# Order of VectorE, GpSimd and ScalarE work in the expert loop of a fused pre-norm layer

## What is computed

```python
def _layernorm(x, axis=-1, eps=1e-05):
    m = jnp.mean(x, axis=axis, keepdims=True)
    v = jnp.var(x, axis=axis, keepdims=True)
    return (x - m) / jnp.sqrt(v + eps)
...
# expert layer: xr = rows of the tokens, sorted by expert; T = 4096, TOPK = 2, E = 8
for e in range(E):
    mask = (bin_ids == e).astype(xr.dtype)[:, None]
    h = jax.nn.gelu(xr @ w1A[e].T @ w1B[e], approximate=False)
    ye = h @ w2A[e].T @ w2B[e]
    out = out + mask * ye
y = jnp.zeros((T, hs), xr.dtype).at[tok].add(flat_w[order][:, None] * out)
...
x = x + attn(layernorm(x))     # the long convolution, with its residual
x = x + ffn(layernorm(x))      # the expert layer
```

## Time and profile before

| what | value |
|---|---|
| median of 3 runs | 1114.91 us (1108.42 to 1119.63) |
| profiled execution, its own time | 1123.56 us |
| its span | 1121.8 us |
| TensorE matmul busy | 908.9 us (81%) |
| VectorE busy | 818.6 us (73%) |
| ScalarE busy | 783.4 us (70%) |
| GpSimd busy | 592.9 us (53%) |
| granted TensorE clock, mean | 0.93 of full |

### The profile page before, as it was taken

One profiled execution on the slowest core, in us unless ns is written; L12 is line 12 of the kernel. 1 busy time (PEld: TensorE's weight loads), 2 busy tenths in 40 slices (PEclk: granted clock), 3 DMA queues, 4 the chain that ended last, 5 costly groups with the idle time before them and its releaser, 6 DMA issues. The chain is left out here.

```text
span 1121.8 us, 32819 instructions
## 1 busy us (share of the span) xinstructions
PE 908.9 (81%) x11452; PEld 765.3 (68%) x11452; DVE 818.6 (73%) x1360; ACT 783.4 (70%) x1151; POOL 592.9 (53%) x642
## 2 busy tenths in 40 slices
PE   3760888888778788998989999899987888885881
PEld 2540676777667677787878788778876777774771
DVE  7878898979789333576756676776667989895891
ACT  3872898979779545655556566566677989896890
POOL 5625986868584133464656575657655323332330
PEclk9995899989989899999999999999998989998996
DMA  9998999999999896999999999899759989999976
GB/s 307 396 400 304 253 253 236 283 226 307 298 284 328 242 274 155 260 256 290 266 249 238 244 240 240 219 235 246 186 123 265 215 216 272 242 294 289 306 183 150
DMA packets 392136, 288.01 MB, mean 257 GB/s; under 512 B 125928, under 2 KB 339592, under 8 KB 391554
## 3 DMA queue, kind: packets, MB, share of 16 engines
q1 hardware_dynamic: 346018, 211.68, 69.1%
q0 software_dynamic: 19520, 36.26, 15.5%
q10 hardware_dynamic: 26528, 39.14, 9.9%
HBM read 197.41 MB, written 100.61 MB: 266 GB/s over the span
## 5 line engine op out<-in xcount | busy, mean ns | idle before, releaser
L1512 PE MATMUL ps<-xn,wb 128*128 128x128 f32 x2048 | 276.7, 291 | 0.0
L1512 PEld LDWEIGHTS ps<-xn,wb 128*128 128x128 f32 x2048 | 252.0, 201 | 17.5 <-issue 3.1
L598 POOL TENSOR_TENSOR cen<-xb,mean 128x512 f32<-128x512 f32 x128 | 143.1, 1119 | 219.2 <-DVE state L1316 142.5
L1114 ACT ACTIVATE cen<-ps 128x1024 f32<-128x1024 f32 x118 | 117.9, 1024 | 149.2 <-PE ps L1607 130.8
L1289 DVE TENSOR_TENSOR xn<-cen,rstd 128x1024 f32<-128x1024 f32 x128 | 174.6, 1364 | 49.7 <-POOL cen L598 37.0
L1607 PE MATMUL ps<-carry,wb 64*128 64x256 f32 x1248 | 163.5, 404 | 30.8 <-DVE carry L1362 25.5
L1499 PE MATMUL ps<-xn,near 128*32 128x128 f32 x2048 | 86.8, 289 | 119.3 <-DVE xn L1289 72.6
L1607 PEld LDWEIGHTS ps<-carry,wb 64*128 64x128 f32 x1248 | 126.0, 198 | 69.8 <-issue 44.7
L1300 DVE TENSOR_TENSOR xb<-xb,ps 128x1024 f32 (+1 forms) x128 | 152.8, 1194 | 9.9 <-PE ps L1524 9.9
L1011 ACT ACTIVATE wb<-wide 32x1024 f32<-32x1024 f32 x126 | 144.6, 1147 | 15.2 <-DMA wide<-taps_d 12.7
L1499 PEld LDWEIGHTS ps<-xn,near 128*32 128x32 f32 x2048 | 52.2, 112 | 142.1 <-issue 65.8
(11 more groups left out here) (179 smaller groups left out, 1349.3 us busy)
## 6 DMA issues: line engine op xcount, KB each, us to landing
xb<-L_attn_x SPq DMA_DIRECT2D x160, 512.0 KB, 9.9
out<-xb SPq DMA_DIRECT2D x72, 512.0 KB, 6.5
xb<-L_attn_x ACTq DMA_DIRECT2D x128, 256.0 KB
out<-xb SPq DMA_DIRECT2D x88, 256.0 KB, 4.7
wb<-L_ffn_w_B SPq DMA_DIRECT2D x78, 256.0 KB
wide<-taps_d SPq DMA_DIRECT2D x63, 256.0 KB, 5.9
dk<-decay_d SPq DMA_DIRECT2D x63, 128.0 KB, 4.8
out<-y_d SPq DMA_DIRECT2D x4, 1536.0 KB, 12.6
```

What stands on the lines that cost most here:

```text
L598: pool.tensor_tensor(cen[:, k, 0:QB // 2].rearrange("p b r d -> p r b d"), unit_view(pool, g, i, k)[:, :, 0:UC // 2] .rearrange("p r (b d) ...
L1114: act.activation(act_at(q, b).rearrange("p f t -> p (f t)"), ps[:, 2 * (b % 2):2 * (b % 2) + 2, :].rearrange("p a t -> p (a t)"), ACT.Gelu ...
L1512: ins = pe.matmul(ps[:, QB * k + b, d * P:(d + 1) * P], wb[:, h, k * QB + b, d, :], xn[:, k, 2 * b + d, :], start=(b > 0 and d == 0), stop ...
```

## The change

VectorE copies the rank result before it takes the token statistics, and it takes the first pair of rows behind the output weight instead of ahead of the token statistics. GpSimd makes the inverse root of tile q+1 at the start of tile q instead of that of tile q+2 at the end of tile q. ScalarE issues the four row loads of tile q+1 behind the last Gelu of tile q, instead of behind `stage_up` in tile q+1.

```diff
--- before.py
+++ after.py
@@ -652,6 +652,8 @@
             def tile(q, m, first, rows):
 
                 k = m % 2
+                if is_in(q, NQ - 1):
+                    deviation(q + 1, 1 - k)
                 if first:
                     gather(2, 0)
                 if isinstance(q, int) and q == NQ - 1:
@@ -667,8 +669,6 @@
                     scatter(p, p % 4)
                 if is_in(q, NQ - 3):
                     gather(q + 3, 1 - k, None if isinstance(q, int) else (m + 3) % 4)
-                if is_in(q, NQ - 2):
-                    deviation(q + 2, k)
                 if isinstance(q, int) and q == NQ - 3:
                     scatter(q - 2, (q - 2) % 4)
 
@@ -680,7 +680,6 @@
             gather(0, 0)
             gather(1, 1)
             deviation(0, 0)
-            deviation(1, 1)
 
             def picked(p):
 
@@ -1091,16 +1090,8 @@
 
             def tile(q, m, first, rows):
 
-                def rows2(i0):
-
-                    for i in range(i0, i0 + 2):
-                        load2((q - ROW0) * LR2 + i, i, (q - ROW0) * 2 + i // 2)
-
                 if is_in(q, NQ - 1):
                     stage_up(q + 1)
-                if rows:
-                    rows2(0)
-                    rows2(2)
                 for b in range(4):
                     if b == 2 and not first:
                         for h in range(2):
@@ -1116,6 +1107,9 @@
                                    ACT.Gelu).then_inc(s_ge, 1)
                     if b == 2 and is_in(q, NQ - 1):
                         turned(q + 1)
+                if not isinstance(q, int) or ROW0 <= q + 1 < ROW0 + TT:
+                    for i in range(LR2):
+                        load2((q + 1 - ROW0) * LR2 + i, i, (q + 1 - ROW0) * 2 + i // 2)
 
             act.wait_ge(s_wc, FC + KC)
             stage_up(0)
@@ -1411,17 +1405,16 @@
                 if is_in(q, NQ - 1):
                     for h in range(2):
                         normal(q + 1, 1 - k, h)
-                if rows:
-                    rows2(q, 0)
-                if is_in(q, NQ - 2):
-                    token_stats(q + 2, k)
                 if first:
                     dve.wait_ge(s_w2b, 32)
                 stage_out(q, e)
                 if rows:
+                    rows2(q, 0)
                     rows2(q, LR2 // 2)
                 if is_in(q, NQ - 1):
                     rank_in_half(q + 1)
+                if is_in(q, NQ - 2):
+                    token_stats(q + 2, k)
                 if not rows and not is_in(q, ROW0 + TT):
                     for _ in range(3):
                         next(spread, None)
```

## The result

The changed kernel takes 1134.3 us in the median of 4 runs (1131.07 to 1135.04), the kernel before 1117.27 us in the median of its 4 (1108.42 to 1123.22). The ratio is 1.0153 with a 95% interval of 1.0079 to 1.0228: slower by about 1.5%. The forecast was 1110, the range went to 1128, so the prediction was wrong, in its sign and in its range.

The account below looks back on a forecast made before the run. It took stalls of 4.48 us a turn above TensorE's floor of 40.20 as what can be won. Seven turns -3.0, the tile ahead -2.5 and the tail +1 made -4.5; on the median 1114.91 this gave 1110, range 1092 to 1128.

Parts of the forecast that it names:

- The mechanism that I named as the cost of the change: At a turn's border: the root waits behind the gather's index copy, so TensorE starts turning tokens 2.8 us late.
- the landing at the border: At turn borders: second gather half's issue to the gather's index copy takes 6.35 us, the mean of seven borders before.
- the slower matmuls behind the stall: At each border: TensorE's matmuls after its late turning cost 0.95 us more; bounds 0 and 1.25.
- what could be won: In the expert loop: stalls above 40.20 us a turn, 4.48 a turn, 31 us over seven.
- The signs: In the loop: rank-copy wait nearly gone, no gathered-token wait, seven normalising stands of 1.4 to 4 us, fourth periods 13 to 14.5.
- Inside a turn: Three of a loop turn's four tiles: 10.05 us each plus 0.1 for VectorE's new order.
- The tile ahead of the loop: The tile before the first loop turn: should take 10.05 us instead of 12.54, so -2.5.
- R+8.95: At a border: TensorE's turning starts 8.95 us after R, the start of an undisturbed rank copy, instead of R+6.15.
- The tail: After the loop: the last root stands behind one more scatter, +1 us, bounds 0 and 3.
- The lengthened landing: At borders: early row loads lengthen the gather's landing to 8.44 us; turn 46.65, total +12.3, 1127 us; chance 0.18.
- The cheap border: At borders: landing 4.96 us, TensorE 1.4 late, matmuls stay fast; turn 41.9, total -21, 1094 us; chance 0.23.
- The chain rival: In GpSimd: each scatter waits for the previous one's landing, a turn takes 45.2 us; +2, 1117 us; chance 0.17.

Follow-up runs that it names:

- e3: The changed kernel with ScalarE's row loads put back behind the weight copy: 1126.0 us, ratio to before 1.0052.
- e2: The kernel before with GpSimd's part alone, the root first in its tile: 1121.2 us, ratio to before 1.0048.
- e11: The changed kernel with VectorE's part undone, root first and early row loads kept: 1131.3 us, ratio to before 1.0117.
- e4: The kernel before with VectorE's new order alone: 1113.1 us, ratio to before 0.9973.
- e1: The changed kernel with GpSimd's root put back at the end of its tile: 1119.5 us, ratio to before 1.0029.
- e13: The kernel before with only both index copies made tile by tile, at the start of each tile: 1104.6 us, ratio to before 0.9875.
- e14: The kernel before with VectorE's new order and both index copies tile by tile, early: 1107.4 us, ratio to before 0.9901.
- e5: The changed kernel with the root at the tile's end and both index copies per tile, behind the landings: 1118.1 us, ratio to before 1.0011.
- e9: The kernel before with ScalarE's early row loads alone: 1117.2 us, ratio to before 1.0018.
- e10: The changed kernel with row loads back behind the weight copy and both index copies per tile, early: 1098.1 us, ratio to before 0.9815.

## Why the prediction was wrong

The mechanism that I named as the cost of the change was the right one; two of its terms were too small (the landing at the border, forecast 6.35, measured 7.33, and the slower matmuls behind the stall, forecast 0.95 a border, measured 1.90), and the account of what could be won was read from the wrong place.

- *The signs.* The wait for L1362 went, VectorE waits for no gathered tokens, the root stands behind L627 and TensorE stands for the normalising seven times, as forecast. But the longest stand is 5.7 us and not 4, the fourth periods are 13.7 to 19.3 and not 13 to 14.5, and one index copy starts at R+10.1.
- *Inside a turn.* Forecast 10.15 a tile, measured (323.00-110.75)/21 = 10.11. The order fits under TensorE, as worked out. The tile ahead of the loop: forecast -2.5, measured -2.4.
- *The landing at the border.* This is the step that failed first. I took 6.35 from the seven borders of before; it was 7.33 in the changed kernel. The early row loads make a good part of the difference: about half by e3 (6.82 with them back), and 5.91 to 7.25 between e2 and e11. They moved further than the 1 us that I had written. At the border of the earlier trace rows they began at 639.85, R+0.36, before; at the same border after they began at 641.43, R-1.45. The second gather half itself is also issued later, R-0.1 in the mean against the R-0.5 that I took, and the steps behind the index copy were 0.3 shorter than forecast. I had this as the slower rival, with 8.44 from one tile, and gave it 0.18. I had named the direction of the row loads and yet took into the forecast the mean of landings that for the most part had no row loads in front of them. The rule of the Trainium skill that I set beside it (DMA: Bandwidth & Descriptors, "Queues, rings and completion order": a DMA engine goes round the queues that have work) agrees with these runs, in which the landing grew by 0.3 to 1.3 us in all four pairs; the size had to be measured.
- *The slower matmuls behind a stall.* Forecast 0.95 a border, from stalls of 2 to 3 us at the up matmuls. Measured: from turning to the next rank copy 5.81 us in the mean instead of 3.91, so 1.90, and 0 to 3.0 at single borders. The stalls were longer (3.9 in the mean against 2.8), and the transposes and down matmuls that follow ran at the lower clock.
- *Together.* Turning at R+10.01 instead of R+8.95 and 1.90 instead of 0.95: a border of 15.82 instead of 13.80, 7 x 2.02 = 14.1 us. The tail cost +2 instead of +1. With -4.5 as the forecast's sum this gives +10.6; the profiled executions differ by 11.4. So with the measured sizes put in, the forecast's own steps come within 0.8 us of the measured difference.
- *The rivals.* The lengthened landing said a turn of 46.65 us and +12; the turn measured 46.14. It was the right case, though with a landing of 7.3 and 1.90 of slower matmuls instead of 8.4 and 1.25. The break-even landing of 6.7 that it gave was not tested as such; e3, with 6.82, came out 0.5% slower, which does not contradict it. The cheap border (4.96 together with no clock loss) did not occur once. The chain rival was wrong for the changed kernel, where the border alone lengthens a turn, but right for V and for V with R (e4, e1): there GpSimd sets the pace.
- *The 1128.* The medians are 17.0 apart, the profiled executions 11.4. The kernel before varies from 1108 to 1123 from run to run, the changed one from 1131 to 1135, and the profiled execution of before was at the upper end. I worked the difference out against this one long execution and carried it over to the median. One execution before has one turn of 40.9 and others of 44.8 to 46.2, so its loss to stalls is itself a sample. That this makes the last 6 us is argued, not shown.
- *What could be won.* The 31 us of stalls exist, but VectorE's order alone wins none of them for certain (e4). The stall at the rank copy was the last place of a chain: the index copy waits for a landing, the next scatter is late, each scatter waits for the one before, the gather behind it is late, then the statistics, then the rank copy. e13 takes the first link away and wins 1.25% without touching VectorE. The links between are read from single rows; e13 tests the first and the last together.

## What to carry to other kernels

Follow a wait back past its releaser, round the loop, to the first link that can't catch up; moving work at the place where the stall shows only moves the stall. When an instruction moves "to the start of the next tile", look at what the program puts between two turns of a loop, since it now stands behind that. A wait that protects a shared buffer against its last reader (here an index table read by DMAs in flight) was cheap to remove with a small ring whose slots are known to be free, with the refill ahead of the other waits and not behind them (e14, 0.9901, against e5, 1.0011; they differ besides in the row loads, which alone showed no change of time in e9). That the indices must be copied at all inside the loop was taken as given; no run here tries without.

## What the runs showed of the hardware

- A gather of 128 rows of 2 KB (indirect, from GpSimd) lands 5.0 to 9.0 us after its issue at the borders of this loop, and the mean over a kernel's borders grew by 0.3 to 1.3 us in four pairs of kernels when only four 256 KB loads on ScalarE's queue started earlier, by 1.2 to 1.8 us in the mean.
- Two stalls of TensorE of about the same length do not cost the same afterwards. In the changed kernel a turning late by 3.1 to 3.2 us was followed by 1.6 us of slower matmuls at three borders, one late by 3.3 by 3.0, one late by 3.7 by none and one late by 3.8 by 3.0. The granted clock of these border periods was 0.88 to 0.89, 0.79, 1.00 and 0.80.
- The 16 DMA engines were busy for 0.91 of the changed kernel's loop and 0.99 of e10's, which moves the same bytes in 289 instead of 323 us; a share of 0.91 was not the limit.
